# A unit matrix in three weight matrices in place of residual adds, and x2 transposed in squares through DRAM

## What is computed

```python
x = x + L0(x)
# L1, L3: W = weights[condition];  einsum('bct,bcd->bdt', x, W)
x = x + L1(x)
# L2: base = x @ W.T; logits = x @ Wr.T + 5 * onehot(lang); top-2, softmax -> gates
#     base + 2 * einsum('bter,bte,eor->bto', x @ A.T, gates, B)
x = x + L2(x)
x = x + L3(x)
```

## Time and profile before

| | |
|---|---|
| runs | 566.25, 568.54, 570.8 us, median 568.54 |
| the profiled execution | 562.91 us, of which the span is 561.1 |
| PE busy | 551.3 us, 98% |
| DVE, ACT, POOL busy | 57%, 36%, 39% |
| DMA engines, 463 to 538 us | busy share 0.33, 110 GB/s |

### The profile page before, as it was taken

One profiled execution on the slowest core, in us unless ns is written; L12 is line 12 of the kernel. 1 busy time (PEld: TensorE's weight loads), 2 busy tenths in 40 slices (PEclk: granted clock), 3 DMA queues, 4 the chain that ended last, 5 costly groups with the idle time before them and its releaser, 6 DMA issues.

```text
span 561.1 us, 8757 instructions
## 1 busy us (share of the span) xinstructions
PE 551.3 (98%) x3224; PEld 499.3 (89%) x3224; DVE 321.4 (57%) x734; ACT 203.1 (36%) x400; POOL 219.0 (39%) x229
## 2 busy tenths in 40 slices
PE   6999999999999999999999999999999999999997
PEld 6889988898989898989898989898989899999995
DVE  6797354545464545454454545454454567777776
ACT  6775232424333333324232323323232533333330
POOL 5752144656565655424141414141420223433430
PEclk9999999999999999999999999999999999999999
DMA  8983356566766666656464646474647611333322
GB/s 294 367 272 138 113 163 197 165 208 191 230 180 218 193 205 195 203 189 180 159 175 159 192 142 201 136 211 134 213 130 227 239 57 58 100 136 122 113 96 75
DMA packets 62666, 97.83 MB, mean 174 GB/s; under 512 B 8352, under 2 KB 32032, under 8 KB 62624
## 3 DMA queue, kind: packets, MB, share of 16 engines
q1 hardware_dynamic: 51600, 60.00, 32.3%
q0 software_dynamic: 10880, 37.23, 22.1%
q10 hardware_dynamic: 144, 0.04, 0.0%
HBM read 74.44 MB, written 22.81 MB: 173 GB/s over the span
## 4 chain that ended last, share of the span: by engine, by line
PE 89%; DVE 4%; DMA 3%; POOL 2%; issue 1%; ACT 0%; SPq 0%; DVEq 0%; ACTq 0%
PE gu_ps L1269 13%; PE gu_ps L1267 13%; PE gu_ps L1268 13%; PE down_ps L1267 8%; PE down_ps L1268 8%; PE down_ps L1269 8%; PE l_ps L1267 5%; PE l_ps L1268 5%; PE l_ps L1269 5%; PE gu_ps L1275 3%; PE gu_ps L1274 3%; POOL a_raw L745 1%; DMA x_res<-act_blocks 1%; PE x2t_ps L1394 1%; DMA a_raw<-a_all,idx_batch 1%
## 5 line engine op out<-in xcount | busy, mean ns | idle before, releaser
L745 POOL DMA_INDIRECT b_sel_raw<-b_gu,idx_rank x48 | 47.5, 990 | 154.7 <-PE gu_ps L1275 144.4
L1267 PE MATMUL down_ps<-wd_sb,act_hl 128*128 128x288 f32 (+1 forms) x352 | 105.1, 299 | 0.5 <-DVE act_hl L1030 0.3
L1268 PE MATMUL down_ps<-wd_sb,act_hl 128*128 128x288 f32 (+1 forms) x352 | 103.8, 295 | 0.0
L1269 PE MATMUL down_ps<-wd_sb,act_hl 128*128 128x288 f32 (+1 forms) x352 | 103.6, 294 | 0.0
L1267 PE MATMUL gu_ps<-w_sb,xt 128*128 128x512 f32 x256 | 102.0, 399 | 0.0
L1269 PE MATMUL gu_ps<-w_sb,xt 128*128 128x512 f32 x256 | 100.4, 392 | 0.0
L1268 PE MATMUL gu_ps<-w_sb,xt 128*128 128x512 f32 x256 | 100.3, 392 | 0.0
L745 POOL DMA_INDIRECT a_raw<-a_all,idx_batch x60 | 65.8, 1096 | 60.3 <-DVE wd_sb L1030 46.3
L1094 DVE TENSOR_TENSOR act<-act,gu_ps 128x512 f32<-128x512 f32 (+1 forms) x47 | 29.8, 633 | 97.4 <-ACT act L863 97.2
L863 ACT ACTIVATE act<-gu_ps 128x512 f32<-128x512 f32 (+1 forms) x47 | 26.1, 555 | 144.4 <-PE gu_ps L1275 144.4
L1267 PEld LDWEIGHTS down_ps<-wd_sb,act_hl 128*128 128x128 f32 (+1 forms) x352 | 66.0, 188 | 2.7 <-DVE act_hl L1030 0.9
(11 more groups left out here) (154 smaller groups left out, 1082.8 us busy)
## 6 DMA issues: line engine op xcount, KB each, us to landing
act_blocks<-act SPq DMA_DIRECT2D x39, 256.0 KB, 4.0
x_res<-act_blocks SPq DMA_DIRECT2D x156, 64.0 KB
xt_raw<-x_t SPq DMA_DIRECT2D x16, 256.0 KB, 5.1
w_sb_raw<-wgu SPq DMA_DIRECT2D x16, 256.0 KB, 7.8
x_res<-x_rows SPq DMA_DIRECT2D x16, 256.0 KB, 3.2
x_after_l<-x_res SPq DMA_DIRECT2D x16, 256.0 KB, 2.0
bd<-bd_hl SPq DMA_DIRECT2D x16, 256.0 KB, 2.2
x<-x_after_l SPq DMA_DIRECT2D x16, 256.0 KB, 2.8
```

Of the source, the lines that this page charges most:

```text
L745: nc.gpsimd.indirect_dma_start(out=dst, out_offset=None, in_=table, in_offset=bass.IndirectOffsetOnAxis(ap=idx, axis=0)).then_inc(s, 16)
L1267: pe.matmul(out_, stationary[0], moving[0], start=start, stop=False, skip_group_check=True)
L1268: pe.matmul(out_, stationary[0], moving[1], start=False, stop=False, skip_group_check=True)
L1269: return pe.matmul(out_, stationary[1], moving[0], start=False, stop=stop, skip_group_check=True)
```

## The change

The constant `unit_ch` (a 32 x 32 unit matrix in each group of 32 rows) is added to the gathered L1 and L3 weights on POOL, and the unit matrix to the four 128 x 128 diagonal pieces of L2's weight (`unit_w2`, also POOL). L1, L2 and L3 then give x plus their product in PSUM, and the three adds on DVE turn into something else: `take_x2` copies (tiles 0 to 2) or transposes in squares (tiles 3 to 15) from PSUM; `high_x3` on ACT and `low_x3`, now on DVE, read L2's PSUM directly; `copy_y` on ACT takes L3's PSUM to `y`. For tiles 3 to 15 the four PE transposes go, and SP stores the squares (`store_x2`) and loads them in four pieces (`load_x2`) into `x2_landed`, from which ACT and DVE split them. `l1` stands three tiles ahead in place of two, x1 is loaded and split four tiles ahead, and `experts(i-1)` lies between two halves of the second `l2_base`.

```diff
@@ sync
             def load_tile(t):
                 sp.wait_ge(s_xout[t % 2], 16 * (t // 2 + 1))
                 if t >= 2:
-                    sp.wait_ge(s_x2, t - 1)
+                    sp.wait_ge(s_x1lo, t - 1)
...
+            def store_x2(t):
+                sp.wait_ge(s_x2, t + 1)
+                if t - 2 >= MOVED_X2:
+                    sp.wait_ge(s_x2in[t % 2], 16 * HC * moved_x2(t - 2))
+                sp.dma_start(x2_scratch[t % 2, :, :], x2_blk[:, t % 2, :]).then_inc(s_x2out[t % 2], 16)
+
+            def load_x2(t):
+
+                if t - 2 >= MOVED_X2:
+                    sp.wait_ge(s_x2tlo, t - 1)
+                sp.wait_ge(s_x2out[t % 2], 16 * moved_x2(t))
+                for j in range(HC):
+                    sp.dma_start(x2_landed[j * CH:(j + 1) * CH, t % 2, :].rearrange("f (b n) -> f b n", b=TB),
+                                 x2_scratch[t % 2, :, j * P:(j + 1) * P].rearrange("(b f) n -> f b n", b=TB)
+                                 ).then_inc(s_x2in[t % 2], 16)
...
+            for k in range(1, NT + 3):
+                if MOVED_X2 <= k + 2 < NT:
+                    store_x2(k + 2)
+                if k + 4 < NT:
+                    load_tile(k + 4)
+                if BD <= k + 5 < NT:
+                    load_bd(k + 5)
+                if k >= 3:
+                    u = k - 3
                     for n, (a, b) in enumerate(pieces(u)):
-                        sp.wait_ge(s_y, u + n + 1)
+                        sp.wait_ge(*((s_y, u + 1) if n == 0 else (s_y2, 1)))
                         sp.dma_start(out[u * P:(u + 1) * P, a:b], y_of(u)[:, a:b]).then_inc(s_out[u % 2], 16)
+                if MOVED_X2 <= k + 2 < NT:
+                    load_x2(k + 2)
@@ gpsimd
+                unit = w13_raw[:, t % 2, :].rearrange("p (m d) -> p m d", d=CH)
+                pool.tensor_tensor(unit, unit, const("unit_ch").unsqueeze(1).to_broadcast([P, 2, CH]),
+                                   ALU.add).then_inc(s_unit, 1)
+                pool.wait_ge(s_unit, t + 1)
...
+            def unit_w2(c):
+
+                pool.wait_ge(s_w[c], 16)
+                at = c * P // HALF * L2_WIDTH[0] + c * P % HALF
+                w = w2ra_raw[:, 1, c, at:at + P]
+                pool.tensor_tensor(w, w, ident, ALU.add).then_inc(s_wunit, 1)
@@ scalar
-            for i in range(NT + 1):
+            for i in range(NT - 2):
                 if i >= 1:
                     high_hgt(i - 1)
-                    if i + 1 < NT:
-                        high_x2t(i + 1)
-                if 1 <= i < NT:
                     exponential(i)
-                if 1 <= i < NT - 1:
+                    high_x2t(i + 1)
+                if i + 4 < NT:
+                    high_x1(i + 4)
+                if i >= 1:
                     high_x3(i - 1)
-                if i + 3 < NT:
-                    high_x1(i + 3)
+                if i >= 2:
+                    copy_y(i - 2)
@@ vector
-            def add_x2(t):
+            def take_x2(t):
                 ve.wait_ge(s_l1, t + 1)
-                if t >= 3:
-                    ve.wait_ge(s_x3, t - 2)
-                ve.tensor_tensor(x2[:, t % 3, :], x1[:, t % 2, :], l1_ps[:], ALU.add).then_inc(s_x2, 1)
+                if t < MOVED_X2:
+                    ve.tensor_copy(x2[:, t % 3, :], l1_ps[:]).then_inc(s_x2, 1)
+                    return
+                if t - 2 >= MOVED_X2:
+                    ve.wait_ge(s_x2out[t % 2], 16 * moved_x2(t - 2))
+                ve.transpose(x2_blk[:, t % 2, :].rearrange("p (j a r) -> p j a r", j=TB, a=HC),
+                             l1_ps[:].rearrange("p (a j f) -> p j a f", j=TB, f=CH)).then_inc(s_x2, 1)
...
                 route_weights(i)
-                add_x3(i - 1)
+                low_x3(i - 1)
                 route_gates(i)
-                add_x2(i + 2)
-                if i >= 2:
-                    add_y(i - 2)
+                if i + 3 < NT:
+                    take_x2(i + 3)
@@ tensor
+            l1(3)
             for i in range(1, NT - 2):
                 l2_base(i, 1)
                 transpose_hg(i - 1)
-                transpose_x2(i + 1)
-                l2_base(i, 0)
+                if i + 1 < MOVED_X2:
+                    transpose_x2(i + 1)
+                l2_base(i, 0, 0, HC // 2)
                 experts(i - 1)
+                l2_base(i, 0, HC // 2, HC)
                 if i >= 2:
                     l3(i - 2)
-                l1(i + 2)
+                if i + 3 < NT:
+                    l1(i + 3)
```

More of the change, by code:

```diff
@@ L368, in bass_conditioned_residual_chain @@
         y = sb("y", [2, H])
+        x2_blk = sb("x2_blk", [2, H])
+        x2_landed = sb("x2_landed", [2, H])
         l1_ps = ps("l1_ps", [H])
@@ L391, in halves, with moved_x2, by_piece, x3_count @@
             return v[:, a:b].rearrange("p (j n) -> p j n", n=HALF)
+        def moved_x2(t):
+            return sum(k % 2 == t % 2 for k in range(MOVED_X2, t + 1))
+        def by_piece(v):
+            return v.rearrange("p (b j r) -> p j b r", b=TB, j=HC)
+        def x3_count(t, n=0):
+            return t - PLAIN + n + 1
         def base_of(t, a, b):
@@ L451, in bass_conditioned_residual_chain @@
         s_x2 = sem("s_x2")
+        s_x2out = [sem(f"s_x2out{i}") for i in range(2)]
+        s_x2in = [sem(f"s_x2in{i}") for i in range(2)]
         s_x2t = sem("s_x2t")
@@ L820, in _ @@
                     block_diagonals(t + 1)
+                if s == STEPS - 2:
+                    for c in range(HC):
+                        unit_w2(c)
                 if s == STEPS - 1:
@@ L824, in _ @@
                     gather_item(("bd", NT - 1))
[L825 to L830, removed]
+            for t in range(2, NT):
+                low_x1(t)
         @block.scalar
@@ L912, in high_x2t @@
             def high_x2t(t):
-                sc.wait_ge(s_x2t, t + 1)
                 if t >= 2:
                     sc.wait_ge(s_base, t - 1)
+                if t >= MOVED_X2:
+                    sc.wait_ge(s_x2in[t % 2], 16 * HC * moved_x2(t))
+                    sc.copy(x2t_hl[:, t % 2, 0, :, :].rearrange("p j (b r) -> p j b r", b=TB),
+                            by_piece(x2_landed[:, t % 2, :])).then_inc(s_x2thi, 1)
+                    return
+                sc.wait_ge(s_x2t, t + 1)
                 sc.copy(x2t_hl[:, t % 2, 0, :, :], x2t_ps[:]).then_inc(s_x2thi, 1)
@@ L926, in high_x3, with copy_y @@
                     sc.wait_ge(s_l3, t - 1)
-                sc.wait_ge(s_x3, t + 1)
-                sc.copy(x3_hl[:, t % 2, 0, :], x3[:, t % 3, :]).then_inc(s_x3hi, 1)
+                sc.wait_ge(s_l2, t + 1)
+                sc.copy(halves(x3_hl[:, t % 2, 0, :], 0, H), base_of(t, 0, H)).then_inc(s_x3hi, 1)
+            def copy_y(t, n=0):
+                if 2 <= t < NT - 1:
+                    sc.wait_ge(s_out[t % 2], 16 * (t // 2))
+                a, b = pieces(t)[n]
+                sc.wait_ge(s_l3, t + n + 1)
+                sc.copy(y_of(t)[:, a:b], l3_of(t, n)).then_inc(s_y, 1)
             def exponential(t):
@@ L970, in _ @@
                         high_x2t(1)
+                        high_x1(3)
                 if 0 <= s - W13_FIRST - 1 < NT:
@@ L1179, in low_hgt, with low_x3, copy_x3, copy_y @@
                                  ALU.subtract).then_inc(s_hgtlo, 1)
-            def add_x3(t):
-                if t >= 3:
-                    ve.wait_ge(s_y, t - 2)
+            def low_x3(t):
+                ve.wait_ge(s_x3hi, t + 1)
+                ve.tensor_tensor(halves(x3_hl[:, t % 2, 1, :], 0, H), base_of(t, 0, H),
+                                 halves(x3_hl[:, t % 2, 0, :], 0, H).bitcast(F32), ALU.subtract).then_inc(s_x3lo, 1)
+            def copy_x3(t):
                 for n, (a, b) in enumerate(pieces(t)):
                     ve.wait_ge(s_l2, t + n + 1)
[L1186 to L1194, removed]
+                    ve.tensor_copy(halves(x3[:, t % 3, :], a, b), base_of(t, a, b)).then_inc(s_x3, 1)
+            def copy_y(t, n):
+                a, b = pieces(t)[n]
+                ve.wait_ge(s_l3, t + n + 1)
+                ve.tensor_copy(y_of(t)[:, a:b], l3_of(t, n)).then_inc(s_y2, 1)
             ve.memset(warm[:], 0.0).then_inc(s_warm, 1)
@@ L1213, in _ @@
                         ve.tensor_scalar(lang5[:], lang5[:], LANG_BIAS, None, ALU.mult).then_inc(s_lang, 1)
-                        add_x2(0)
+                        take_x2(0)
                         for n in range(HC // 2):
@@ L1218, in _ @@
                         route_top(0)
-                        add_x2(1)
+                        take_x2(1)
                         low_w2(HC)
@@ L1224, in _ @@
                         low_x2t(1)
+                        take_x2(2)
                     if job == ("x1", NT - 1):
                         route_gates(0)
-                        add_x2(2)
+                        take_x2(3)
                 if s == 4:
```

65 lines of the change are left out of this document (38 added, 27 removed).

## The result

The changed kernel takes 578.14 us (median of six runs, 574.08 to 580.04), the kernel before, run beside it, 569.39 (six runs, 566.25 to 570.86). The ratio is 1.0152, with a 95% interval of 1.0107 to 1.0197. I had predicted 571.2 us, +2.7, and given "slower by over 1%" a chance of 0.25. The profiled execution took 574.08 us, 11.2 more than that of before; its span is 572.3.

What follows compares the result with a forecast made beforehand. TensorE was taken to bound the kernel before; after the change, eleven turns of 6.70 us make hg(13) 4.0 us late and a shorter tail returns 1.3, so 2.7 more on 568.54 gives 571.2 us. Range: 565.5 to 578.4.

Steps and rivals of the forecast that it cites:

- the ring: Second stage: x2 store, x1 load, ACT's x1 then x3 split, `low_x3`, gates, `take_x2`, next store; 6.70 us a turn, eleven turns.
- ACT's waits: Second stage, ahead of the split of x1: ACT waits 0.5 to 1.5 us for the x1 load in each iteration.
- One sign: TensorE, second stage: waits for hg in front of its transposes, which stand 6.7 us apart up to tile 11.
- TensorE's gain: Second stage, tiles 3 to 15: four x2 transposes leave TensorE, 0.43 us an iteration, 5.6 us in all, leaving 5.78.
- From there no load of x1 is left and TensorE paces again: Behind the transpose of hg(11) at 538.0: hg(12) follows 5.78 us later, hg(13) 5.78 - 0.69 after that.
- hg(11): End of the eleven turns: its transpose starts about 0.6 us ahead of the end of `take_x2(14)`, at 538.0.
- 2.85 for every landing: Second stage, x1 load on SP's queue: time to land taken as 2.85 us in each turn, from a median of 2.8.
- rival 2: Same turns with slow x1 landings behind long issues: decides from 6.98 us a turn, 574.2 us; up to 578.4; chance 0.20.
- a clock under 1.00: TensorE's granted clock in the second stage: a value under 1.00 would mean something was left out; no size given.
- the first take: Start of the eleven turns: `take_x2` for tile 3, whose store is the first, ends at 464.9.
- the tail: What is left of the program behind hg(13): 1.3 us shorter together, from last-tile transposes, two gaps and the last copies.
- the likeliest case: Second stage: turns of 6.35 to 6.97 us, giving 567.4 to 574.2 us; chance 0.58.

Runs made afterwards that it cites:

- experiment 1: Changed kernel with ACT splitting x3 (`high_x3(i-1)`) ahead of x1 (`high_x1(i+4)`); 571.09 us, ratio 1.0016 to the kernel before.
- Experiment 8: Changed kernel with one edit, DVE's `low_x3(i-1)` ahead of `route_weights(i)`; ratio 1.0228 to the kernel before.
- Experiment 3: Changed kernel with x3 split before x1 on ACT, x1 load before x2 store on SP, `low_x3` before `route_weights` on DVE; 566.76 us, ratio 0.992.
- experiment 5: Experiment 3 with x2 of all tiles transposed on TensorE again and none sent through DRAM; 564.93 us, ratio 1.0004 to the kernel before.
- experiments 6 and 9: Changed kernel, POOL's `low_x1` held until hg of tile t-4; in 6 SP loads x1 before storing x2 (0.996), in 9 ACT splits x3 before x1 (0.9988).
- experiment 4: Changed kernel with SP issuing the load of x1 behind `load_bd` and the store of the output; 597.45 us, ratio 1.0495 to the kernel before.

## Right and wrong, step by step

**Right: the ring, its members and its length.** The turn was to be 6.70 us; the six undisturbed ones are 6.62 to 6.75. ACT's waits came as promised (but for one of 1.8 us), and DVE's for the split of x3; the landings of x1 are 2.7 / 2.8 / 3.5 where I had 2.7 to 3.0. One sign came at another place: TensorE waits in front of `l2_base(i, 1)`, for `low_x3`, and not in front of the transpose of hg. That is the first trace of the step that failed, below. Experiments 1 and 8 show the ring from both sides: take the load off the path and the loss goes; put 0.56 us more on it and each turn grows by about 0.5.

**Right: TensorE's gain, nearly.** 0.37 us in an iteration, not 0.43, and a pace of 5.85, not 5.78 (experiments 3 and 5). It is only had when both rings are out of the way.

**Wrong: "From there no load of x1 is left and TensorE paces again ... at 5.78".** It doesn't. The last transposes of hg in the changed kernel:

```profile
544.49 0.27 PE L1506 MATMUL hgt_ps<-ident_sb,hg 128*128 128x128 f32 x1
...
550.56 0.27 PE L1506 MATMUL hgt_ps<-ident_sb,hg 128*128 128x128 f32 x1
...
556.64 0.27 PE L1506 MATMUL hgt_ps<-ident_sb,hg 128*128 128x128 f32 x1
```

6.07 us each, and experiments 6 and 9 show 6.06 nearly all along without the load ring. The step I left out: `low_x3` is now DVE's, and TensorE's 12 matmuls of `l2_base(i, 1)` wait for it. So: `low_x3(i-1)`, 12 matmuls, transpose of hg, its split on ACT and DVE, `route_top`, the exponential, `low_x2t`, `route_weights`, `low_x3(i)`. Between the last two transposes above:

```profile
551.16 0.29 DVE L1265 TENSOR_TENSOR hgt_hl<-hgt_ps,hgt_hl 128x128 fp32r<-128x128 f32 x1 [1.04 <-ACT hgt_hl L979]
...
553.96 0.69 DVE L1270 TENSOR_TENSOR x_hl<-l_ps,x_hl 128x512 fp32r<-128x512 f32 x1
```

```profile
554.75 0.39 PE L1351 MATMUL l_ps<-w2ra_hl,x2t_hl 128*128 128x328 f32 x1 [0.68 <-issue]
```

From the transpose to the low part of hg 0.60, from there to `low_x3` 2.80, to the first of the 12 matmuls 0.79, to the next transpose 1.89: 6.08 us. I costed what left TensorE and what was added to DVE, and the load ring between them, but not the ring that the moved split closes with TensorE. Experiment 3 moves the three small operations of `route_weights` out of it, and it falls under TensorE's pace.

The same omission moved hg(11). I set its transpose 0.6 ahead of the end of `take_x2(14)`; behind the wait for `low_x3` and 12 matmuls it comes 544.49 - 544.08 = 0.4 after the store that this take releases. The DVE timeline shows the like: `take_x2` at 502.30, the transpose of hg at 503.43.

**Mis-sized: 2.85 for every landing.** The 11 turns took 544.08 - 467.60 = 76.5 us, where I had 73.7. Four turns carry it, and three of them begin with a long issue of the load, of this kind:

```profile
468.02 1.20 SPq L678 DMA_DIRECT2D x<-x_after_l  x1
...
489.74 0.92 SPq L678 DMA_DIRECT2D x<-x_after_l  x1
...
537.09 0.77 SPq L678 DMA_DIRECT2D x<-x_after_l  x1
```

These loads land in 3.5, 3.2 and 3.5 us, and their turns are 7.48, 7.09 and 7.43 (a fourth issue, of 0.51, has a landing of 3.0 and a turn of 6.96). That is rival 2, in three turns of eleven. The mean turn of 6.95 stays just under the 6.98 at which I had put that rival's decision. Before, three of twelve issues were as long (0.91 to 1.17) and cost nothing: the distances were 6.20 to 6.21 all along, since nobody on the path waited for the load.

**Left out: the clock.** The fourth is the second turn, 7.52 us. The longest wait of TensorE, 2.04 us, comes with the first turn, and behind it (start, length, line):

```profile
473.54 0.39 PE L1351 MATMUL l_ps<-w2ra_hl,x2t_hl 128*128 128x328 f32 x1 [2.04 <-issue]
...
474.22 0.31 PE L1352 MATMUL l_ps<-w2ra_hl,x2t_hl 128*128 128x328 f32 x1
...
475.26 0.47 PE L1351 MATMUL l_ps<-w2ra_hl,x2t_hl 128*128 128x328 f32 x1
475.53 0.47 PE L1352 MATMUL l_ps<-w2ra_hl,x2t_hl 128*128 128x328 f32 x1
```

The starts stand 0.27 apart in place of 0.15, and the window from 474.60 on has a clock of 0.50. In this turn ACT doesn't wait for the load at all: `high_x1` follows directly on ACT's work before it, at 478.25. It is the second ring, with half of its 12 matmuls at 1.2 GHz (2.54 us from the first to the transpose of hg, 473.54 to 476.08, where 1.87 is usual) and a held product:

```profile
479.43 0.87 DVE L1248 TENSOR_TENSOR route<-route 128x1 f32<-128x1 f32 x1
```

Together 6.06 + 0.67 + 0.71 = 7.4 us: the clock and POOL share that turn about equally. The prediction named a clock under 1.00 as the sign of something left out, and so it was: here a stall of TensorE was paid for again at the lower clock.

**The tally** on the profiled execution, 565.6 predicted and 574.1 got, so 8.5 us:
- 2.7: the first take ends at 467.57, not 464.9. About 2.0 of it is older than the second stage: the last transpose of `td` in L0 starts at 462.01, not at 459.97. The rest lies at 465.06, where a gate operation (L1253) took 1.17 us in place of the 0.57 that it took before (0.28 is usual), beside two `low_x1` of POOL (463.67 to 466.20)
- 2.8: eleven turns, 76.5 us in place of 73.7
- 1.0: the place of hg(11) in the turn
- 1.3: hg(12) and hg(13), 6.07 + 6.08 in place of 5.78 + 5.09
- 0.8: from hg(13) to the end 15.7 us in place of 14.9. Before it was 16.2, so the tail got 0.5 shorter, and I had put 1.3

Most of the 2.0 us of L0 can't come from the unit adds on POOL, the only work that the change adds to L0. The first of these (L836) starts at 96.9 us, and the second transpose of `td` already stands 1.45 us later than before (75.69 against 74.24). Behind the fifth (164 us before) the lateness stays at 2.03 to 2.06, though the adds go on until 235 us. So at most 0.6 us lie where they could be the cause. In the profiles of the nine experiments, whose L0 is the same, the last transpose of `td` comes 0.6 to 8.3 us later than before. In the two latest, experiments 1 and 3, 6.9 and 6.4 us are there at the first one: TensorE has one wait of 4.5 and of 5.7 us there, ending at 26.3 and 26.7 us, and a stretch at 1.2 GHz goes with it. The kernel before has one profile only, but its runs spread as well (562.67 to 570.36 us on one chip). So a part of the 11.2 us between the two profiled executions is chance, and the medians' 8.7 is the better number. What starts the early waits stays open.

**The number.** Without those 2.0 us the miss is 6.5 us: 571.2 + 6.5 = 577.7, beside a median of 578.14. That the two agree to 0.4 us is partly luck, since only one execution was profiled and the six spread over 6 us; and that 578.14 still lies in my range is luck too, for the upper end stood for slow landings in every turn, and three of eleven were slow. My chances went by a mean of the load ring alone. Each of the missing terms lengthens the time, and the likeliest case stood 3.0 us under the bound to "slower"; so they were enough to change the verdict, not the mechanism.

## What to carry to other kernels

When an order is changed, walk every ring that each moved instruction closes, not only the longest that was found, and also those that hold no DMA: here two rings lay at 6.06 and 6.70 us over a pace of 5.85; with the 6.06 us ring cut alone the kernel lost 2.3% against before, with the 6.70 us ring cut alone it stood between +1.1 and -0.4%. Put no wait for a load ahead of work that another engine waits for. The repair was three swaps of neighbours, and it turned +1.5% into -0.8%.

## What the hardware showed

**A small DVE operation can be held by POOL.** L1248 took 0.16 alone and 0.70 to 0.88 beside `low_x1` (once 0.36); L1255 0.17 and 1.23 to 1.30. Those shown ended 0.02 us behind POOL's operation, and the reciprocal L1247, with one operand in SBUF, wasn't slowed beside the same `low_x1`. The Trainium skill, "SBUF — State Buffer", section "🔬 SBUF: two separate sides", says that a DVE operation with two SBUF inputs and a GpSimd operation that reads SBUF share a port pair by an exclusive lock, held for the whole instruction. The trace agrees, with these numbers. L1253, a tensor-scalar operation on a constant with both scalars in SBUF, was held as well (0.28 and up to 1.23); no run tells which of its operands does it.

**A stall of TensorE can cost more than its length, but needn't.** The idle time of 2.04 us in the changed kernel was followed by 3.3 us at the 1.2 GHz level, and in experiment 4, with waits up to 3.3 us, the clock of the stage is 0.91. Experiment 8 has two waits of 1.98 us. Behind the one that ends at 473.31 the starts of its matmuls stand 0.27 apart again; behind the one that ends at 488.66 the clock stays at 1.00. The waits of 0.5 to 1.4 us elsewhere in the changed kernel left the clock at 1.00.

**The landing of a load isn't a constant.** The same 256 KB load took 2.7 to 2.8 us as second in SP's turn with a short issue (the changed kernel), 3.4 to 5.0 as fourth (experiment 4), and a median of 3.7 (2.7 to 5.4) in experiment 5, where SP issues it 0.43 us behind the store of the output. The place isn't all: in experiment 1 one load took 4.5 us as second, with an issue of 0.38. Why stays open.
